# Three staging buffers instead of seven for the V tiles of a cross-attention

## What is computed

```python
q = x @ Wq.T
k_raw = context @ Wk.T
v_raw = context @ Wv.T
# 32 heads of 16; k and v are interleaved in the concatenation of k_raw and v_raw
q = _rmsnorm(q)
k = _rmsnorm(k)
scores = jnp.einsum('bhnd,bhmd->bhnm', q, k) * scale
attn = jax.nn.softmax(scores, axis=-1)
out = jnp.einsum('bhnm,bhmd->bhnd', attn, v)
```

## Time and profile before

| | |
|---|---|
| time, median of 3 runs | 2594.69 us (2594.05 to 2601.93) |
| profiled execution: time, span | 2594.69 us, 2593.0 us |
| TensorE busy | 2404.5 us, 93% |
| VectorE busy | 1357.4 us, 52% |
| ScalarE busy | 1347.1 us, 52% |
| GpSimd busy | 909.5 us, 35% |
| stores vd<-A_c_vt | 104, 136 KB each |

### The profile page before, as it was taken

One profiled execution on the slowest core, in us unless ns is written; L12 is line 12 of the kernel. 1 busy time (PEld: TensorE's weight loads), 2 busy tenths in 40 slices (PEclk: granted clock), 3 DMA queues, 4 the chain that ended last, 5 costly groups with the idle time before them and its releaser, 6 DMA issues. The chain is left out here.

```text
span 2593.0 us, 39125 instructions
## 1 busy us (share of the span) xinstructions
PE 2404.5 (93%) x15376; PEld 1547.4 (60%) x15376; DVE 1357.4 (52%) x2114; ACT 1347.1 (52%) x1708; POOL 909.5 (35%) x592
## 2 busy tenths in 40 slices
PE   7996999999999999999997899998799999999897
PEld 5885644444444444444334555555588888888786
DVE  5566534434344434443414655555655666665775
ACT  4231467667776777767993444333322455555221
POOL 1224754555456445554112433331140121121220
PEclk9998999999999999999999999999899999999999
DMA  5002675576538654764636000010261466665330
GB/s 178 17 1 78 196 212 143 133 195 170 143 104 220 160 150 105 205 180 126 165 84 211 2 1 18 1 50 28 91 214 55 144 213 234 214 222 174 119 124 33
DMA packets 208007, 331.46 MB, mean 128 GB/s; under 512 B 71312, under 2 KB 125840, under 8 KB 207632
## 3 DMA queue, kind: packets, MB, share of 16 engines
q1 hardware_dynamic: 190608, 256.99, 35.0%
q0 software_dynamic: 15056, 68.03, 7.9%
q10 hardware_dynamic: 2160, 3.93, 0.5%
HBM read 241.53 MB, written 99.42 MB: 131 GB/s over the span
## 5 line engine op out<-in xcount | busy, mean ns | idle before, releaser
L938 ACT ACTIVATE A_c_prob<-c_psum 128x1024 f32<-128x1024 f32 x832 | 787.0, 1029 | 282.2 <-PE c_psum L1188 271.8
L864 POOL TENSOR_TENSOR c_rr<-c_ms,c_half 128x32 f32<-128x32 f32 (+1 forms) x72 | 372.5, 5176 | 424.2 <-DVE c_ms L955 424.2
L1197 PE MATMUL c_psum<-A_c_prob,c_vq 128*17 128x512 f32 x3328 | 415.5, 599 | 8.6 <-DVE c_oT L1092 8.4
L134 PE MATMUL c_psum<-R_c_w,S_c_c 128*128 128x512 f32 x1248 | 314.0, 401 | 0.7 <-DVE S_c_c L966 0.6
L1188 PE MATMUL c_psum<-c_qq,c_kq 64*128 64x512 f32 x1664 | 288.7, 438 | 23.3 <-ACT A_c_prob L938 11.3
L134 PEld LDWEIGHTS c_psum<-R_c_w,S_c_c 128*128 128x128 f32 x1248 | 227.9, 189 | 121.9 <-issue 41.6
L1188 PEld LDWEIGHTS c_psum<-c_qq,c_kq 64*128 64x128 f32 x1664 | 136.8, 185 | 173.2 <-ACT A_c_prob L938 92.7
L134 PE MATMUL m_psum<-R_m_t,m_up_hi 128*128 128x256 f32 (+1 forms) x1104 | 203.5, 285 | 23.9 <-DVE R_m_t L2313 23.9
L2358 PE MATMUL m_psum<-A_m_dn_hi,A_m_a 128*128 128x512 f32 (+1 forms) x628 | 205.4, 396 | 10.2 <-DVE A_m_a L2167 10.2
L995 DVE COPY Q_c_unit<-c_psum 128x256 f32<-128x256 f32 x89 | 37.8, 425 | 334.4 <-PE c_psum L134 334.4
L1616 DVE TENSOR_REDUCE s_topx<-s_psum 128x4 f32<-128x2048 f32 (+1 forms) x64 | 95.5, 1493 | 172.7 <-PE s_psum L1719 168.0
(11 more groups left out here) (296 smaller groups left out, 4329.2 us busy)
## 6 DMA issues: line engine op xcount, KB each, us to landing
c_kq<-kd SPq DMA_DIRECT2D x248, 208.0 KB, 6.0
kd<-S_c_t SPq DMA_DIRECT2D x96, 256.0 KB, 3.9
Q_c_raw<-in_ctxT SPq DMA_DIRECT2D x89, 256.0 KB, 4.9
qd<-A_c_q SPq DMA_DIRECT2D x64, 256.0 KB
c_qq<-qd SPq DMA_DIRECT2D x64, 256.0 KB, 3.3
vd<-A_c_vt SPq DMA_DIRECT2D x104, 136.0 KB, 3.8
c_vq<-vd SPq DMA_DIRECT2D x31, 442.0 KB, 9.0
R_m_hs<-slots SPq DMA_DIRECT2D x23, 512.0 KB, 7.5
```

The costliest lines, as they stand in the source:

```text
L134: mm = pe.matmul(out, a(c), b(c), start=first and i == 0, stop=last and i == len(terms) - 1)
L864: pool.tensor_tensor(rr[:, unit % RB, 0:n], ms[:, unit % RB, 0:n], half[:, 0:n], ALU.pow).then_inc(s_r, 1)
L938: act.activation(prob[:, t % PB, 2 * (u % 2):2 * (u % 2) + 2, :], score_banks[u % 3], ACT.Exp, scale=XD ** -0.5).then_inc(s_ex, 1)
L1197: mm = pe.matmul(o_bank[32 * j:32 * j + VW, :], vq[:, q % 2, kt, j, :], prob[:, t % PB, j, :], start=kt == 0, stop=kt == CT - 1)
```

## The change

The staging tile `vt` gets 3 buffers in place of 7. Tiles 0 to 11 of a half use buffer 0 or 1 by their parity, and the last tile buffer 2. The semaphores that count landed stores become three, the waits before a quad load go over three, and the memsets of the ones columns are made for three buffers.

```diff
-    CB, PB, RB, VB = 4, 3, 4, 6
+    CB, PB, RB = 4, 3, 4
...
-    v_buf = lambda n: VB if n % CT == CT - 1 else (n - n // CT) % VB
+    v_buf = lambda n: 2 if n % CT == CT - 1 else n % CT % 2
...
-        vt = A.tile("c_vt", at, VB + 1, HH, VW)
+        vt = A.tile("c_vt", at, 3, HH, VW)
...
-        s_kst, s_vst, s_quad = m.sem("kst0", "kst1"), m.sem(*[f"vst{i}" for i in range(VB + 1)]), m.sem("quad0", "quad1")
+        s_kst, s_vst, s_quad = m.sem("kst0", "kst1"), m.sem("vst0", "vst1", "vst2"), m.sem("quad0", "quad1")
...
-                for i in range(VB + 1):
+                for i in range(3):
                     tiles = [n for n in range(h * CT + last) if v_buf(n) == i]
                     if tiles:
                         sp.wait_ge(s_vst[i], 16 * len(tiles))
...
-                    for i in range(VB + 1):
+                    for i in range(3):
                         sp.wait_ge(s_vst[i], 16 * sum(1 for n in range(2 * B * CT) if v_buf(n) == i))
...
-            pool.memset(vt[:, 0:VB, :, XD:VW], 1.0).then_inc(s_const, 1)
-            pool.memset(vt[:, VB, :, XD:VW], 0.0).then_inc(s_const, 1)
+            pool.memset(vt[:, 0:2, :, XD:VW], 1.0).then_inc(s_const, 1)
+            pool.memset(vt[:, 2, :, XD:VW], 0.0).then_inc(s_const, 1)
             pool.wait_ge(s_const, 3)
-            pool.memset(vt[0:LAST, VB, :, XD:VW], 1.0).then_inc(s_const, 1)
+            pool.memset(vt[0:LAST, 2, :, XD:VW], 1.0).then_inc(s_const, 1)
```

## The result

The changed kernel takes 2611.72 us (median of 8 runs, 2604.54 to 2615.58), the kernel before 2596.34 us beside it (8 runs, 2593.75 to 2603.52). The ratio is 1.0051, 95% interval 1.0039 to 1.0063: slower by 13 us, where 10.5 us was forecast.

A forecast was written before the change was run, and what follows sets the result against it. TensorE bounds the cross-attention, so only waits reaching it count. 1.4 (prologue), 4.2 (tile 21), 2.6 (tile 89), 1.5 and 0.8 (clock) gave 10.5 us on 2594.69, thus 2605.2 us; range 2597.5 to 2612, forecast alone 2599.4 to 2609.

The forecast's parts named there:

- Bound, and which stores are late: Cross-attention: TensorE is the bound; 12 of 104 tiles short, by 0.4 to 6.2 us; not all waits reach TensorE.
- memsets and semaphores: Smaller memsets, four fewer semaphores, fewer waits before loads: a gain of 0.1 us at most, taken as 0.
- Tile 21: Copy waits for tile 19's store, delaying normalisation and transposes by 5.1 us; less the 0.88 us c_vq wait, +4.2 us.
- The clock's part: TensorE at the 1.2 GHz level after new idle time: +1.5 us at tile 21, +0.8 us at tile 89.
- Tile 89: Copy waits for tile 87's store, delaying mean squares, root, normalisation and TensorE: +2.6 us, plus 0.8 us for the clock.
- Prologue: Copies of tiles 13 and 14 wait for stores of 10 and 11; first scores at about 303.1, +1.4 us.
- tile 17: VectorE waits until 337.1, while TensorE idles until 336.03 for c_vq and then has other work: 0, at most 1 us.
- Tiles 33 to 37: TensorE moves about 1.2 us and tile 37 waits 5 us, both into the 3.70 us c_vq wait before 553.43: 0.
- The sum: Prologue 1.4, tile 21 4.2, tile 89 2.6, clock 1.5 and 0.8: 10.5 us, nothing given back.
- The signs named: First scores, tile 21 transposes, idle near 1114 us, shorter c_vq wait near 553 us, constant shift from 600 to 1060 us.
- The later stages: Behind the cross-attention: they begin after it, unchanged in themselves, so its end is later by the whole sum.
- The rival of two buffers being enough: Cross-attention: late landings are chance or copies sit in idle time; only the prologue's 1.4 us stays, 2596; chance 0.27.

The follow-up runs named there:

- after_again: The changed kernel profiled once more, with no timing; its value copy of tile 92 came 12.3 us later than in the trace before, counted from tile 0.
- map_only: The kernel before with only the two-buffer parity assignment of V tiles; seven buffers, semaphores, waits and large memsets stay; ratio 1.0043 to the kernel before.
- warm: The kernel before with the parity assignment, plus extra unread TensorE matmuls ahead of the transposes behind tiles 21 and 90; ratio 1.0036 to the kernel before.
- act_all_two: The changed kernel with value stores issued from ScalarE's queue instead of SyncE's, three buffers; ratio 0.9974 to the kernel before.
- free_21_89: The kernel before with the parity assignment, but tiles 21 and 89 have buffers of their own; ratio 1.0004 to the kernel before.
- free_13_14: The kernel before with the parity assignment, but tiles 13 and 14 have buffers of their own; ratio 1.0039 to the kernel before.
- before_again: The kernel before, unchanged, profiled once more, with no timing; its value copy of tile 92 came 2.8 us later than in the trace before.

## Why the prediction was right, point by point

**Bound, and which stores are late: right in the main.** Twelve tiles were forecast as short. Eight of them waited, for 22.7 us in all: 7, 13, 17, 21, 33, 37, 85 and 89. Tiles 34 to 36 did not, as the forecast says further on, nor did 14, whose copy follows the late one of 13. Tiles 18, 19 and 20 were not forecast and waited for 1.0 us together. In after_again seven copies waited, all of them forecast. map_only shows that the assignment is all, as forecast for memsets and semaphores.

**Tile 21: 4.2 + 1.5 = 5.7 us forecast, 4.3 to 7.2 measured.** TensorE idled for 5.57 us (3.84 to 5.57 in the profiles of this assignment), the wait of 0.88 us fell away, as forecast. The clock's part was mis-sized: the slow stretch lasted 6.8 us, not 3.4, and 7.2 - (5.57 - 0.88) = 2.5 us went there. The forecast sized this term on an idle time of about 4 us, though its own row had the transposes 5.1 us late with no idle time before them. warm bears the size out: 2.9 us less behind the transposes without the slow stretch. In after_again the slow stretch was 3.4 us, and 4.3 - (3.84 - 0.88) = 1.3 us went there.

**Tile 89: 2.6 + 0.8 = 3.4 us forecast, 5.2 measured.** The chain through mean squares, root and normalisation came as written: the sums of the next quad were 2.7 us later by themselves. The rest, 5.2 - 2.7 = 2.5 us, was lost behind them at the half clock, where the forecast took the middle of "slow stretch or none".

**Prologue: 1.4 us forecast, none left.** The first scores came 1.2 us later than before (304.99 - 301.74, less the 2.04 of tile 0), right as written in its number. That it is the wait for the stores which costs this is not shown: in act_all_two, where no copy waits, the first scores are 1.8 us later than in the trace before, for c_vq. The step that failed is that the delay would stay: a slow stretch of 10.2 us, where the kernel before has 3.4, brought it to 3.5 us, and TensorE's wait for the second quad's c_vq then shrank from 3.56 to 1.65 us, and the slow stretch behind that wait did not come. The forecast noted that wait as cover for tile 17 and did not let it take up the prologue's delay; it looked for such waits only behind 553 us. free_21_89 keeps the prologue's wait and loses 0.4 us in all.

**Tiles 33 to 37: 0 forecast, 0 measured**, +1.9 us up to tile 36 and back by tile 40. The wait for c_vq shrank from 3.70 to 1.35 us, and the slow stretch that follows it in the kernel before, 3.4 us from 554.4 us on, did not come. The forecast's "go into that idle time" was not quite so for tile 37: behind it TensorE idled for 1.06 us at 573 us and 0.80 us at 576 us, and the missing slow stretch paid for that. Tile 17 cost nothing, as forecast.

**The sum.** 10.5 us forecast, 12.1 in the profile of the cross-attention. The two clock terms were too small by 2.7 us, the prologue's too large by 1.4. free_21_89 settles the whole: the two stalls named make the loss. That the sum came so close is in part luck: the two errors point opposite ways, and the steps at tiles 21 and 89 differ by some 3 us between two executions of the same kernel. The median of 2611.72 us lies just inside the range, which went up to 2612.

**The signs named.** The first scores came at 302.95 (304.99 less the 2.04 of tile 0; 303.1 forecast), the transposes of tile 21 5.6 us late (5 forecast), the wait for c_vq near 553 us shrank, the shift was 6.3 to 7.2 us from tile 40 to 88 (5 to 8 forecast) in map_only and the changed kernel (4.4 to 4.5 in after_again). TensorE's idle time near 1114 us came in two pieces of 2.38 and 2.04 us, not in one of 3 us.

**The later stages** were forecast unchanged. Their 8.4 us in the first profile are for the most part not of the change: the same code is between 2.0 us shorter and 5.1 us longer in the other profiles (3.3 in after_again), and the timed 13 us leave about 1 us beside the 12.1 of the cross-attention. What makes this part longer or shorter stays open.

**The rival of two buffers being enough** is what an estimate of 2.3 us a store would give, by the Trainium skill, "DMA: Bandwidth & Descriptors", "Anatomy of one DMA — SWDGE (gpsimd) path". The page fits this for transfers that GpSimd issues, and the stores here are SyncE's. The trace agrees for stores with nothing ahead, which took 1.7 to 2.2 us. But here the landing time alone does not decide, the time from copy to issue does: 12.1 us for tile 19.

## What to carry to other kernels

The number of staging buffers has to cover the time from the copy to the store's landing at its longest, and with stores and loads in one in-order queue that is set mostly by what stands ahead of the store, not by the store. Read it per tile, as copy start against the landing of the store that holds the buffer, and then ask for each late one whether the bound engine is waiting there anyway. Before adding buffers, look whether the stores can be issued from a queue with idle time: here that made two rotating buffers faster than six had been, and six faster too, so the gain is the queue's and not that of the number of buffers.

## What was not expected of the hardware

The length of the slow stretch (granted clock 0.50) behind TensorE's idle time. After 3.56 us of idle time it was 3.4 us; after 5.57 us, 6.8 us; after 4.02 us before the first scores, 10.2 us, in which TensorE was waiting for ScalarE between its scores. After 3.84 us in after_again it was 3.4 us, and after 4.64 us at tile 21 of free_13_14 also 3.4 us. Shorter idle times can have one too: 2.23 us before scores of the second quad in before_again, 1.53 us in after_again near 1112 us, each with 3.4 us behind it, while 1.65 and 1.35 us in the changed kernel and 3.04 us in act_all_two, waits for the second or the seventh quad's values, had none. So the length of the idle time alone did not tell what follows. At tile 21 the stall of 5.57 us cost 2.5 us beyond its own length and that of 3.84 us cost 1.3: the idle time alone is too low an estimate of a stall.

The time that one and the same load takes to arrive: TensorE's wait for the seventh quad's values was 3.70 us in one execution of the kernel before and 6.34 us in another.
